# Opening of the FFN reordered, early loads spread over two batches, first weight block split into tiles

## What is computed

```
x = layernorm(x + mixer(x))        # Mamba2-like: in_proj 512 -> 2048, conv of 4 taps, silu,
                                   # x_proj, dt, chunked state scan, gate, out_proj
x = layernorm(x + block_ffn(x))    # prob = softmax(x Wr + br) over 16 blocks of 128 hidden units,
                                   # top 4 kept: y = gelu(x W1) * mask, then W2
x = layernorm(x + attention(x))    # linear attention
x = layernorm(x + experts(x))      # 8 experts, gated, with low-rank additions
```

## Time and profile before

| | |
|---|---|
| three runs | 2356.95, 2358.25, 2360.74 us; median 2358.25 |
| the profiled execution | 2356.86 us, span 2355.1 us |
| PE busy | 2267.4 us (96% of the span) |
| DVE, ACT, POOL busy | 1575.6, 889.1, 758.4 us |
| bytes moved | 154.36 MB, mean 66 GB/s |

### The profile page before, as it was taken

How to read it: one execution, slowest core, us unless ns; L and a number is a source line. 1 busy time by engine, 2 the same in 40 slices (tenths; PEclk the granted TensorE clock), 3 DMA queues, 4 the chain that set the end, 5 groups by cost and what they waited for, 6 DMA issues and landing times.

```text
span 2355.1 us, 30907 instructions
## 1 busy us (share of the span) xinstructions
PE 2267.4 (96%) x10746; PEld 1861.6 (79%) x10746; DVE 1575.6 (67%) x2392; ACT 889.1 (38%) x1441; POOL 758.4 (32%) x570
## 2 busy tenths in 40 slices
PE   8899999999989999999999899999999899999997
PEld 6787788888867888888877688777778778888885
DVE  5557777777758855674455666667677886777665
ACT  4456333333334322322232444234344444444441
POOL 0002544444412222341111533224233543333331
PEclk9999999999999999999999999999999999999998
DMA  5646222222132100000000211221111021111110
GB/s 205 218 141 201 63 72 71 71 71 71 55 110 100 36 19 19 23 1 19 1 1 27 81 53 56 81 81 61 47 54 54 27 90 54 53 54 53 53 36 36
DMA packets 90567, 154.36 MB, mean 66 GB/s; under 512 B 6224, under 2 KB 55376, under 8 KB 83808
## 3 DMA queue, kind: packets, MB, share of 16 engines
q1 hardware_dynamic: 90464, 153.02, 19.4%
HBM read 113.68 MB, written 39.32 MB: 65 GB/s over the span
## 4 chain that ended last, share of the span: by engine, by line
PE 61%; DVE 6%; issue 2%; ACT 1%; POOL 1%; DMA 0%; POOLq 0%; DVEq 0%; ACTq 0%; SPq 0%
PE attn_pvk L1197 4%; PE attn_pvk L1199 4%; PE attn_pvk L1198 4%; PE attn_pq L1197 2%; PE attn_pq L1198 2%; PE attn_pq L1199 2%; PE attn_pv L1197 2%; PE attn_po L1197 2%; PE attn_po L1198 2%; PE attn_po L1199 2%; PE attn_pv L1199 2%; PE attn_pv L1198 2%; PE attn_pv L85 2%; PE attn_pv L87 2%; PE attn_pv L86 2%
## 5 line engine op out<-in xcount | busy, mean ns | idle before, releaser
L2570 DVE TENSOR_TENSOR moe_a_lo<-moe_up_raw,moe_a_hi 128x512 fp32r<-128x512 f32 x192 | 182.7, 967 | 154.8 <-ACT moe_a_hi L2033 154.7
L1915 POOL TENSOR_TENSOR moe_h_lo<-moe_c_t,moe_h_hi 128x512 fp32r<-128x512 f32 x96 | 128.3, 1336 | 356.8 <-ACT moe_h_hi L2033 356.7
L1197 PE MATMUL attn_pvk<-moe_b_hi,moe_a_hi 128*128 128x512 f32 x512 | 200.8, 392 | 13.8 <-ACT moe_c_last L2159 5.8
L1199 PE MATMUL attn_pvk<-moe_b_hi,moe_a_lo 128*128 128x512 f32 x512 | 199.4, 389 | 0.0
L1198 PE MATMUL attn_pvk<-moe_b_lo,moe_a_hi 128*128 128x512 f32 x512 | 199.3, 389 | 0.0
L2033 ACT ACTIVATE moe_c_t<-attn_pvk 128x512 f32<-128x512 f32 x192 | 113.2, 596 | 186.5 <-PE attn_pvk L1199 184.5
L1305 POOL TENSOR_TENSOR ffn_h_lo<-ffn_h_f,ffn_h_hi 128x512 fp32r<-128x512 f32 x64 | 89.9, 1405 | 254.1 <-ACT ffn_h_hi L1360 254.1
L2085 ACT ACTIVATE moe_c_t<-moe_c_t 128x512 f32<-128x512 f32 x96 | 60.4, 629 | 241.6 <-DVE moe_c_t L2642 241.6
L1507 DVE SCALAR_TENSOR_TENSOR all_acc<-attn_pvk,ffn_wts,all_acc 128x512 f32<-128x512 f32 x128 | 91.2, 749 | 89.0 <-PE attn_pvk L87 88.8
L2033 ACT ACTIVATE moe_a_hi<-moe_up_raw 128x512 fp32r<-128x512 f32 x192 | 116.0, 624 | 56.4 <-POOL moe_up_raw L1885 56.4
L1197 PEld LDWEIGHTS attn_pvk<-moe_b_hi,moe_a_hi 128*128 128x128 f32 x512 | 96.2, 188 | 37.6 <-issue 11.0
(11 more groups left out here) (497 smaller groups left out, 6564.4 us busy)
## 6 DMA issues: line engine op xcount, KB each, us to landing
moe_up_raw<-in_e_up SPq DMA_DIRECT2D x28, 1024.0 KB, 5.8
moe_dn_raw<-in_e_dn SPq DMA_DIRECT2D x28, 512.0 KB, 3.7
xh<-mix_out_hi SPq DMA_DIRECT2D x32, 256.0 KB, 2.6
zs<-mix_out_z SPq DMA_DIRECT2D x32, 256.0 KB, 3.2
xl<-mix_out_lo SPq DMA_DIRECT2D x32, 256.0 KB, 3.4
mix_x<-xh SPq DMA_DIRECT2D x16, 512.0 KB, 4.2
mix_x<-xl SPq DMA_DIRECT2D x16, 512.0 KB, 5.3
mix_z_raw<-zs SPq DMA_DIRECT2D x16, 512.0 KB, 3.9
```

What stands on the lines that cost most here:

```text
L1197: pe.matmul(out, lh, rh, start=first, stop=False, skip_group_check=True)
L1199: return pe.matmul(out, ll, rh, start=False, stop=True, skip_group_check=True)
L1915: tt(h_lo[:, m, tok], src, raw(h_hi[:, m, tok]), ALU.subtract).then_inc(s_hlo, 1)
L2570: tt_(a_lo[q][:], src, raw(a_hi[q][:]), ALU.subtract).then_inc(s_alo, 1)
```

## The change

Five edits, none of which changes what is computed:

1. The first weight block is loaded and split in tiles. Tile 0 (128 of the 512 columns) is a transfer of its own between the second and third x chunk, and the other three are one transfer. ACT and DVE split tile 0 ahead of x, and tiles 1 to 3 behind it. PE's first tile waits for x a quarter at a time and for its own weight tile. ACT runs one silu on a column of `ident` first.
2. The early loads are issued one per step in batches 1 and 2 (`ahead` of SP), in ten transfers of 512 KB. SP's loop over batches is unrolled.
3. The results turned in the last chunk use nine banks, as `RESULT_BANKS` lists them. Ten tiles stand ahead of the last out-projection, two behind.
4. `logT` lies where `h_lo` will be. The down weights are therefore loaded at once at the FFN's start, and split (`down_high`, `down_low`) before the first hidden tile.
5. PE starts the up products of token block 0 before batch 3's logits. Between them stand the turning of the logits of chunks 0 to 11 (into `pu[3]`) and of 12 to 15 (into `pd[0]`). The softmax is done for batches 0 to 2 at once and then for batch 3. The ranks of batch 0 come before the first down product; those of the other batches stay in tt = 1 to 3, split in smaller steps.

```diff
+        RESULT_BANKS = SPARE + SPARE[0:3] + (pd[:, 2], pd[:, 3]) + SPARE[3:5]
+        AHEAD_OF_OUT = 10
...
             for c in range(CPB):
                 sp.dma_start(x_tok[:, 0, c], t["x"][0, c * P:(c + 1) * P, :]).then_inc(s_x0[c], 16)
-            load_w(0)
+                if c == 1:
+                    sp.dma_start(w_raw[:, 0, :, 0:P], t["in_w"][:, 0, :, 0:P]).then_inc(s_w0, 16)
+            sp.dma_start(w_raw[:, 0, :, P:TPG * P], t["in_w"][:, 0, :, P:TPG * P]).then_inc(s_w[0], 16)
...
+            def ahead(i):
+                if i < STAGED:
+                    sp.dma_start(stage(i), t["x_wx"][:, i]).then_inc(s_early, 16)
+                elif i < STAGED + 2:
+                    k0 = (i - STAGED) * IT // 2
+                    sp.dma_start(stage_bc[:, k0:k0 + IT // 2], t["x_wbc"][:, k0:k0 + IT // 2]).then_inc(s_early, 16)
...
                     if j:
                         store_lo(b, j - 1)
+                    if 0 < b < LASTB:
+                        ahead((b - 1) * IT + j)
...
-            with sp.Fori(1, LASTB) as b:
+            for b in range(1, LASTB):
                 batch(b)
...
+            act.wait_ge(s_ident, 2)
+            nc.scalar.activation(out_z[:, 0, 0:1], ident[:, 0:1], ACT.Silu)
+            hi_of_first_w(0)
             hi_of_x(0)
-            hi_of_w(0)
+            for m in range(1, TPG):
+                hi_of_first_w(m)
...
-                if i >= 5:
+                if 5 <= i < 8:
                     pe.wait_ge(s_rlo, i - 4)
+                if i == 8:
+                    pe.wait_ge(s_g, NCH)
+                if i >= 10:
+                    pe.wait_ge(s_rlo, i - 6)
...
-    logT = dn_raw[0:2 * NE]
+    logT = log_all[0:2 * NE]
+    EARLY = LASTB * CPB
...
         sp.dma_start(rb[:], t["f_rb"]).then_inc(s_small, 16)
+        sp.dma_start(dn_raw[:], t["f_dn"][0]).then_inc(s_ld, 16)
         sp.wait_ge(s_up0, 16)
         sp.wait_ge(s_x3, 16)
-        sp.wait_ge(s_wts, 1)
-        sp.dma_start(dn_raw[:], t["f_dn"][0]).then_inc(s_ld, 16)
...
+        for f in range(F):
+            pe.wait_ge(s_ulo, f + 1)
+            pe.wait_ge(s_lgT, f + 1)
+            up(0, 0, f)
+            if f == 0:
+                turn_logits(0, EARLY, pu[LASTB])
+            if f == 1:
+                logits(LASTB)
+            if f == 2:
+                turn_logits(EARLY, NCH, pd[0])
...
             pe.wait_ge(s_hlo, m + 1)
             pe.wait_ge(s_dlo, F * u + f + 1)
+            if start:
+                pe.wait_ge(s_lgc, 2)
...
+        on_tokens(0, EARLY, pu[LASTB], 1)
+        down_low(0, F - 1)
+        softmax(0, EARLY, 1)
+        for part in range(4):
+            ranks(0, part)
+        on_tokens(EARLY, NCH, pd[0], 2)
...
+                    if first and tt:
+                        if tt == 2 and f == 0:
+                            softmax(EARLY, NCH, 2)
+                        ranks(tt, f)
```

More of the change, by code:

```diff
@@ L820, in step @@
                 else:
-                    for i in range(KT, 2 * KT):
+                    for i in range(KT, AHEAD_OF_OUT):
                         turn_result(i)
@@ L835, in step @@
                 if not left:
-                    for i in range(2 * KT, 3 * KT):
+                    for i in range(AHEAD_OF_OUT, 3 * KT):
                         turn_result(i)
@@ L900, in batch @@
                     for kt in range(KT):
+                        if first and m == 0:
+                            pe.wait_ge(s_xlo, kt + 1)
                         ins = product(pe, acc[:, m % 4],
@@ L1155, in batch @@
                 lo_of_out(b, IT - 1)
+            lo_of_first_w(0)
             lo_of_x(0)
-            lo_of_w(0)
+            for m in range(1, TPG):
+                lo_of_first_w(m)
             lo_of_w(1)
@@ L1304, in unit @@
                     pool.wait_ge(s_hhi, m + 1)
+                    if first and tt == 0:
+                        pool.wait_ge(s_wts, 1 if f < LASTB else 2)
                     nc.gpsimd.tensor_tensor(h_lo[:, f], h_f[:, f % 2], raw(h_hi[:, f]), ALU.subtract).then_inc(s_hlo, 1)
@@ L1339, in scalar, with down_high, weights_exp @@
             up_high(0, f)
+        def down_high(u, f):
+            act.wait_ge(s_ld, 16 * u + 16)
+            nc.scalar.activation(dn_hi[:, f], dn_raw[:, f], ACT.Copy).then_inc(s_dhi, 1)
+        def weights_exp(chunks, n):
+            act.wait_ge(s_z, n)
+            nc.scalar.activation(pr[:, chunks], lg[:, chunks], ACT.Exp).then_inc(s_e, 1)
         for b in range(LASTB):
             turned_logits(b)
+            down_high(0, b)
         for kt in range(KT):
@@ L1360, in unit @@
                     nc.scalar.activation(h_hi[:, f], h_f[:, f % 2], ACT.Copy).then_inc(s_hhi, 1)
-                    if tt == 0:
-                        act.wait_ge(s_ld, 16 * u + 16)
-                        nc.scalar.activation(dn_hi[:, f], dn_raw[:, f], ACT.Copy).then_inc(s_dhi, 1)
+                    if tt == 0 and not first:
+                        down_high(u, f)
                     if last and tt:
@@ L1368, in unit @@
                                              ACT.Copy).then_inc(s_whi, 1)
-                    if first and f == 0:
-                        act.wait_ge(s_z, tt + 1)
-                        nc.scalar.activation(pr[:], lg[:], ACT.Exp).then_inc(s_e, 1)
+                    if first and tt == 1 and f == 0:
+                        weights_exp(slice(EARLY, NCH), 2)
         units(act, unit)
@@ L1419, in unit @@
                     m = F * NB * u + F * tt + f
+                    if first and tt == 0:
+                        continue
                     if tt == 0:
                         pe.wait_ge(s_ulo, F * u + f + 1)
-                    if not (first and m < F):
-                        pe.wait_ge(s_hf, m - F + 1)
-                    for kt in range(KT):
-                        ins = product(pe, pu[f], (up_hi[:, f, kt], up_lo[:, f, kt]),
-                                      (xc_hi[:, tt, kt], xc_lo[:, tt, kt]), kt == 0, kt == KT - 1)
-                    ins.then_inc(s_up, 1)
-                    if not (first and tt == 0):
-                        down(m - F, f, (tt - 1) % NB, u - 1 if tt == 0 else u, first and m == F)
+                    pe.wait_ge(s_hf, m - F + 1)
+                    up(u, tt, f)
+                    down(m - F, f, (tt - 1) % NB, u - 1 if tt == 0 else u, first and m == F)
         units(pe, unit)
```

137 lines of the change are left out of this document (81 added, 56 removed).

## The result

The changed kernel takes 2335.33 us (median of 4 runs, 2333.71 to 2337.03) against 2358.67 for the kernel before: ratio 0.9899, interval 0.9887 to 0.9911. A second comparison on another occasion gave 2335.61 against 2358.03, ratio 0.9910 (0.9897 to 0.9924). The forecast was 2335.1 us. The profiled execution's span fell from 2355.1 to 2332.4 us, 22.7 us.

A forecast was written before the change was run, and what follows sets the result against it. PE, busy 96% of the span, was taken as the bound, so its idle stretches could be won. 3.3 + 7.6 + 1.2 + 11.0 = 23.1 us gave 2335.1 us from a median of 2358.25; 8-in-10 range 2331 to 2341.

The forecast's parts named there:

- Start: Batch 0, edit 1: first taps start at 17.0 instead of 20.28 us, gaining 3.3 us (bounds 2.4 and 5.0).
- The landing: Batch 0: the second weight block's arrival hardly moves; 0.2 us added for the small rows of tile 0.
- Batch 1: Batch 1, edit 2: PE's 5.5 us wait behind early loads and 2.1 us of lower clock go, 7.6 us.
- the rival of loads that don't fit: Batch 1: stores and load together run under 241 GB/s, ACT waits each step, 2342.7 us; chance 0.05.
- the slower case: Batch 1: stores and load together fall below about 180 GB/s, 2365 us; chance 0.04.
- Mixer's end: Last out-projection, edit 3: two of DVE's four tiles behind it move ahead, gaining 1.2 us (bounds 0 and 1.3).
- The cover that the prediction asked for: Mixer's end: two added tiles on PE (0.9 us) stand in its `g_lo` wait; without it up to 0.5 lost.
- FFN's opening: FFN's start, edits 4 and 5: PE reaches block 1's second step 11.0 us earlier (bounds 4 and 11.3).
- The masks' part: FFN's opening: batch 0's masks ready early end PE's wait at the first `add_down` and lower clock, 6.9 us.
- The order's: FFN's opening: ups fill PE's waits for DVE's split and the last logits; up 3 ends 4.1 us earlier.
- POOL and DVE: FFN's opening, rival: they hold each other, masks come later, the FFN gains 5.5 us, 2340.6 us; chance 0.12.
- My condition: Wrong if PE waits over 2 us between the named places, or 0.43 us distances remain except behind the barrier.

The follow-up runs named there:

- s1b: Changed kernel with second weight block split behind the first step's convolution, and SP marking output buffers free before its loads: 2335.85 us, ratio 0.9906.
- u2: Changed kernel with edit 2 undone (the 5 MB of early loads in a row after batch 0 again): 2341.26 us, ratio 0.9915.
- m1: Changed kernel with two early loads a step in the first five steps of batch 1, instead of one in ten: 2335.17 us, ratio 0.9907.
- warm: Changed kernel with ten more matmuls of 512 columns ahead of the barrier before the FFN: 2335.39 us, ratio 0.9908.
- e4: Kernel before with edit 4 alone (logits in `h_lo`'s place, down weights loaded at the FFN's start, split where before): 2357.13 us, ratio 1.0003.
- f2: Changed kernel with DVE computing the ranks of batch 0 twice: 2342.71 us, ratio 0.9944.

## Why the prediction was right

- **Start, 3.3 us.** 3.7 measured at PE's position in batch 1. The step was right: the first product is 4.5 us earlier (5.0 forecast), the first taps start at 16.90 (17.0 forecast) and are held by the second weight block (s1b moves them by moving it), and what the taps don't give comes back as waits of 1.5 us in all. The landing moved no more than the 0.2 us allowed: ACT began to split the second block at 12.75, 12.59 before.
- **Batch 1, 7.6 us.** 7.7 measured from before to after, 6.8 by u2. The mechanism is as forecast, and m1 shows that the rival of loads that don't fit, and the slower case with it, was further off than its chances say: two loads a step fit too.
- **Mixer's end, 1.2 us.** 1.2 measured. The cover that the prediction asked for, PE's wait for `g_lo`, was there.
- **FFN's opening, 11.0 us.** 9.7 in the first trace; over the eight traces with the new FFN as it is, other than warm, 9.6 to 11.1, mean 10.3, against the mean of before and e4. The masks' part is right, 6.9. The order's is smaller than forecast: the first down product comes 30.1 us after the first transpose in before and 25.8 to 27.4 in the eight traces, which is 3.4 us by the mean and 2.8 in the first trace, where 4.1 was forecast. What the sum left out is the lower clock behind the barrier: by the granted clock it ended 4.0 us after the first transpose in the trace of before and 6.0 us after it in the one of after. The last transpose started 9.0 and 10.1 us after the first, which is 1.1 of the missing 1.3; the rest are the switches between the groups, for which the sum had 0.1 us.
- **POOL and DVE.** The contact came, but beside the path. In the kernel after:

```profile
701.50 2.54 POOL L1349 TENSOR_TENSOR ffn_h_lo<-ffn_h_f,ffn_h_hi 128x512 fp32r<-128x512 f32 x2 [0.19 <-ACT ffn_h_hi L1416]
...
700.19 1.17 DVE L1576 TENSOR_SCALAR ffn_wts<-ffn_sel 128x64 f32<-128x64 f32 x1
701.40 0.22 DVE L1547 COPY ffn_wts<-attn_pvk 128x64 f32<-128x64 f32 x1
701.66 0.22 DVE L1548 TENSOR_TENSOR ffn_wts<-ffn_wts,attn_pvk 128x64 f32<-128x64 f32 x1
701.91 0.96 DVE L1550 TENSOR_TENSOR ffn_wts<-ffn_wts,ffn_rb 128x64 f32<-128x64 f32 x1
```

  The bias took 0.96 us beside POOL and 0.22 in f2 with POOL idle; the copy and the sum, which read PSUM, took 0.22 beside POOL. The Trainium skill ("SBUF — State Buffer", Who interferes with whom) says that a VectorE instruction with two inputs in SBUF contends with a GpSimd one that reads SBUF, and one with at most one input there does not, outside the modes that use both of VectorE's port pairs. The trace agrees for the bias, the copy and the sum. The last operation of the ranks, with one input in SBUF, took 1.17 us beside POOL and 0.20 in f2 with POOL idle; whether it ran in such a mode no run shows. So POOL did hold the copy back, by 1 us. The sum that PE waits for ended at 701.88, and PE wanted it at 703.70. The slack was 1.8 us.
- **The total is right partly by luck.** The mechanisms as measured sum to 3.7 + 7.7 + 1.2 + 10.3 = 22.9 us; 23.1 were forecast, and the medians of the two comparisons give 23.3 and 22.4. In the first pair of traces the FFN gave 1.3 us less than forecast, the clock took 1.8 us in chunk 0, and the layers behind the FFN gave 2.7, a distance that lies anywhere between 1265.6 and 1269.7 us over the 14 traces. My condition, that no stretch of 0.43 us distances be left between the places named apart from the one behind the barrier, failed: in chunk 0, which I had not looked at, there were two (225 to 229 and 241 to 246 us). PE also waits over 2 us there, 4.4 us for `mix_a_rep` in 13 of the 14 traces, that of before among them.

## What to carry to other kernels

Cost a change at PE's positions. The distance between two landmarks comes back within 0.1 us as long as the clock doesn't fall between them (345.74 to 345.78 us in ten traces, from the first down product to the attention), where four runs of the changed kernel spread over 3.3 us; over a stretch in which the clock falls, one trace is off by 1.6 to 3.9 us, and it takes several. Compare medians only within one occasion. Ask at each gain what the next holder of the same chain is (here the second weight block, and behind it SP's marks in a queue of loads), since it decides how much of an earlier start is kept. A busy share of the transfers near 1 does not mean that they are full; adding a load tells.

## What was not expected of the hardware

The same instructions lost 0 to 3.9 us to the lower clock in one stretch of 47 us, from one trace to another, behind the same idle time of 1.96 to 1.98 us. In 4 of the 14 traces the clock fell behind 16 small products, where PE had not waited at all. With an idle time of 1.9 instead of 4.2 us at the barrier the transposes behind it ran at the full clock, in the one trace that has it, and the clock fell 5.1 us after the first of them, behind a second wait. What decides whether it falls was not settled.
